# Splitting the router's gate of an attention and expert kernel into three rounds of 4, 2 and 2 batches

## The reference, cut to what matters

```python
x = x + attention(layernorm(x), ctx)          # x: (8 batches, 128 tokens, 256); 32 heads, 8 groups of keys
flat = layernorm(x).reshape(1024, 256)
xm = layernorm(x).mean(axis=1)                # one row for each batch
h1 = gelu(xm @ te_W1.T + te_b1)
task_dist = softmax(h1 @ te_W2.T + te_b2)     # 4 domains
dom = task_dist @ affinity.T                  # 64 values for each batch
logits = flat @ Wr.T + 0.5 * dom              # 64 experts
_, idx = top_k(logits + router_bias, 4)
w = softmax(logits)[idx]; w = w / (w.sum() + 1e-8)
out = sum of w * (silu(x @ Wg[e]) * (x @ Wu[e])) @ Wd[e] over the 4 experts e of a token
out = out + two shared experts of width 256, for every token
x = x + out
```

## Time and profile before

| | |
|---|---|
| median of three executions | 324.55 us (321.69 to 328.14) |
| the profiled execution | 324.12 us, its span 322.1 us |
| PE busy | 250.3 us, 78% of the span |
| DVE, ACT, POOL busy | 176.0, 137.1, 98.7 us |
| mean granted clock of PE | 0.896 |

### The profile page before, as it was taken

The page is one execution under the profiler, slowest core; times in us unless marked ns, Lnnn a source line. Parts: engine busy times, 40 slices in busy tenths (PEclk is TensorE's granted clock), DMA queues, the critical chain, the costliest instruction groups (busy, mean ns, idle before and its releaser), DMA issues.

```text
span 322.1 us, 6518 instructions
## 1 busy us (share of the span) xinstructions
PE 250.3 (78%) x2298; PEld 180.0 (56%) x2298; DVE 176.0 (55%) x441; ACT 137.1 (43%) x326; POOL 98.7 (31%) x188
## 2 busy tenths in 40 slices
PE   3687999999999879998699602999999949759100
PEld 2555567677676555886478401877777716535000
DVE  4468678788787634842058590134355403523943
ACT  2237779678678562433010500533466503512000
POOL 5316404203202011167701772000000262272472
PEclk9999999999999987999689955899999976996855
DMA  6903347437569053662200225589999974763642
GB/s 172 314 7 98 133 135 260 141 126 255 188 215 381 4 195 128 265 228 114 98 19 17 98 98 173 171 246 266 296 277 312 287 225 125 221 177 118 217 143 81
DMA packets 43871, 56.55 MB, mean 176 GB/s; under 512 B 4348, under 2 KB 39744, under 8 KB 42816
## 3 DMA queue, kind: packets, MB, share of 16 engines
q1 hardware_dynamic: 32064, 39.37, 37.8%
q0 software_dynamic: 3072, 8.39, 8.0%
q10 hardware_dynamic: 8704, 8.39, 7.5%
HBM read 34.12 MB, written 22.02 MB: 174 GB/s over the span
## 4 chain that ended last, share of the span: by engine, by line
PE 58%; issue 25%; DVE 6%; DMA 4%; POOL 2%; ACT 2%; SPq 1%; POOLq 0%; ACTq 0%; DVEq 0%
PE bank L1547 12%; PE bank L1172 10%; PE banks L1563 7%; PE banks L1323 6%; PE banks L1333 5%; PE bank L1313 5%; DMA before_wlo<-in_L_xattn_Wfc 3%; PE bank L1176 2%; PE banks L1172 2%; DVE xb_all L1145 2%; PE bank L1466 2%; PE bank L1484 2%; POOL after_whi L596 1%; DVE mx L808 1%; PE bank L1468 1%
## 5 line engine op out<-in xcount | busy, mean ns | idle before, releaser
L808 DVE TENSOR_REDUCE mx<-bank 128x4 f32<-128x512 f32 x64 | 41.8, 684 | 13.8 <-PE bank L1313 12.9
L596 POOL DMA_INDIRECT after_whi<-y_slots,idx x24 | 23.0, 960 | 82.2 <-DMA y_slots<-after_x 66.3
L1121 DVE TENSOR_TENSOR after_x<-bank,after_x 128x128 f32<-128x128 f32 x32 | 9.3, 292 | 69.0 <-ACT after_x L745 60.8
L641 ACT ACTIVATE before_w<-banks 128x512 f32<-128x512 f32 x64 | 38.3, 617 | 19.8 <-PE banks L1323 19.8
L740 ACT ACTIVATE after_wlo<-bank 128x512 f32<-128x512 f32 x32 | 19.1, 598 | 43.3 <-PE bank L1172 38.2
L587 POOL DMA_INDIRECT x_slots<-x_all,idx x28 | 27.2, 972 | 22.7 <-DVE idx L933 14.4
L1313 PE MATMUL bank<-before_w,before_w 128*128 128x512 f32 x64 | 27.7, 458 | 2.7 <-ACT before_w L635 1.4
L1323 PE MATMUL banks<-before_w,before_w 128*128 128x512 f32 x64 | 28.1, 448 | 0.7 <-ACT before_w L641 0.5
L1172 PE MATMUL bank<-ident,xt_all 128*128 128x128 f32 x64 | 13.3, 330 | 18.3 <-DMA xt_all<-x_slots 17.2
L1547 PE MATMUL bank<-after_wlo,after_wlo 128*64 128x64 f32 x512 | 22.6, 241 | 5.1 <-issue 5.1
L1547 PEld LDWEIGHTS bank<-after_wlo,after_wlo 128*64 128x64 f32 x512 | 19.4, 152 | 9.4 <-issue 7.8
(11 more groups left out here) (217 smaller groups left out, 525.8 us busy)
## 6 DMA issues: line engine op xcount, KB each, us to landing
x_slots<-before_sil SPq DMA_DIRECT2D x8, 1024.0 KB, 4.5
w_all<-gate_up SPq DMA_DIRECT2D x8, 1024.0 KB, 4.8
y_slots<-after_x ACTq DMA_DIRECT2D x32, 256.0 KB
w_all<-down SPq DMA_DIRECT2D x8, 512.0 KB, 5.9
xt_all<-x_slots SPq DMA_DIRECT2D x16, 256.0 KB, 4.1
after_so_far<-x_slots SPq DMA_DIRECT2D x8, 256.0 KB
after_sel<-x_slots SPq DMA_DIRECT2D x8, 256.0 KB
after_sil<-in_L_ffn_Wd SPq DMA_DIRECT2D x32, 64.0 KB
```

The lines of the kernel that those rows point to most:

```text
L596: nc.gpsimd.indirect_dma_start(out=got[b % 4][:, k * D:(k + 1) * D], out_offset=None, in_=y_slots[0:last * QROWS], in_offset=bass.Indirect ...
L641: nc.scalar.activation(Pr[g], ST_ps[g % 2][:], exp, scale=SCALE).then_inc(a_exp, 1)
L808: nc.vector.tensor_reduce(mx[par][:, J * g:J * g + J], S_ps[g % 2][:].rearrange("p (j t) -> p j t", j=J), AX_X, ALU.max).then_inc(v_max, 1)
```

## The change

- The gate works in rounds of 4, 2 and 2 batches. The first round is now settled inside attention: its domain steps in step 6, its choice, ranks and all placing in step 7. The domain steps of the second round run in steps 7 and 8, its choice in step 9. The third round follows with the rest of the second after the loop.
- Router logits are computed and summed for one batch in each of the steps 2 to 9 instead of for four batches together.
- For batches 6 and 7 DVE computes mean and variance of the rows itself and POOL only takes the power; PE turns their rows at the head of steps 8 and 9.
- POOL issues the four indirect DMAs of batch 0 in step 8, and the other 28 after the loop, round by round.
- PE starts the shared experts later: gate product 0 in two parts in step 8, units 1 and 2 in step 9 between the gate's products.
- ACT no longer copies the first round's counts and ranks out of PSUM (`counted`), and three rounds need three gelu and three exp steps of the domains instead of two. The PSUM regions of the gate's products move accordingly.

The core of the diff (every hunk on shapes and PSUM regions alone is cut):

```diff
+ROUNDS = ((0, 4), (4, 6), (6, 8))
+LAST_ROUND = len(ROUNDS) - 1
...
+GATE = tuple((LOGITS, b) for b in range(4)) + named(0, DOMAINS) + ((LOGITS, 4),) + named(0, ("logits",) + CHOICE) + (
+        placing(0, 0) + placing(0, 1) + placing(0, 2) + ((LOGITS, 5),) + placing(0, 3)) + (
+        named(1, DOMAINS) + ((LOGITS, 6),) + named(1, ("logits",) + CHOICE) + placing(1, 0) + named(2, DOMAINS[:3])) + (
+        placing(1, 1) + named(2, DOMAINS[3:5]) + placing(1, 2) + placing(1, 3) + named(2, DOMAINS[5:]) + ((LOGITS, 7),)) + (
+        named(2, ("logits",) + CHOICE) + placing(2, 0) + placing(2, 1) + placing(2, 2) + placing(2, 3)) + (
...
-                if has(n - 2):
+                if has(n - 2) and n < B:
                     k = n - 2
                     pool.wait_ge(v_stats, k + 3)
                     wait(pool, v_x2n, k)
                     deviations(LN2, LN2 + 1, LN_STEPS * (k + 2))
+                if has(n - 2) and n >= B:
+                    pool.wait_ge(v_ln, 2 * (n - B + 1))
+                    nc.gpsimd.tensor_tensor(mean_var[:, 2:3], mean_var[:, 1:2], minus_half[:, 0:1], ALU.pow).then_inc(g_rstd, 1)
...
+                if n_is(n, B):
+                    pool.wait_ge(zero_in, 128)
+                    pool.wait_ge(g_x2, 4)
+                    pool.wait_ge(v_gate, gate_step(("rows of the slots", 0)))
+                    scatter(0)
...
-            pool.wait_ge(zero_in, 128)
-            pool.wait_ge(g_x2, B - 1)
-            for b in range(B):
-                if b % HB == 0:
-                    pool.wait_ge(v_gate, gate_step(("rows of the slots", b // HB)))
+            def scatter(b):
+
                 for k in range(TOPK):
...
+
+            pool.wait_ge(g_x2, B - 1)
+            for h in range(len(ROUNDS)):
+                pool.wait_ge(v_gate, gate_step(("rows of the slots", h)))
+                for b in range(max(1, ROUNDS[h][0]), ROUNDS[h][1]):
+                    scatter(b)
...
-                    if g == 7 and n_is(n, B - 2):
+                    if g == 7 and n_is(n, B - 3):
                         hidden_of_domains(0)
-                    if g == 1 and n_is(n, B - 1):
+                    if g == 4 and n_is(n, B - 2):
                         exp_of_domains(0)
-                    if g == 0 and n_is(n, B):
-                        act.wait_ge(pe_rank, 1)
-                        nc.scalar.activation(counted, bank[1][:], copy).then_inc(a_rank, 1)
-                    if g == 3 and (n_is(n, B) or n_is(n, B + 1)):
-
-                        silu(n - B, (n - B) % 2)
+                    if g == 7 and n_is(n, B - 1):
+                        hidden_of_domains(1)
+                    if g == 3 and n_is(n, B):
+                        exp_of_domains(1)
+                    if g == 5 and n_is(n, B):
+                        silu(0, 0)
+                    if g == 3 and n_is(n, B + 1):
+                        rows_out(B - 1)
...
-            silu(2, 0)
-
-            hidden_of_domains(1)
-
-            exp_of_domains(1)
+            hidden_of_domains(LAST_ROUND)
+            exp_of_domains(LAST_ROUND)
+            for v in range(1, EARLY):
+                silu(v, v % 2)
...
+
+                dve.wait_ge(v_stats, k + 3)
+                nc.vector.bn_aggr(mean_var[:, 0:2], stats[:, LN2].rearrange("p a s -> p (a s)")).then_inc(v_ln, 1)
+                dve.wait_ge(v_ln, 2 * (k - B + 2) + 1)
+                nc.vector.tensor_scalar(mean_var[:, 1:2], mean_var[:, 1:2], EPS, None, ALU.add).then_inc(v_ln, 1)
+                dve.wait_ge(g_rstd, k - B + 3)
+                dve.wait_ge(pe_XT, k)
+                dve.wait_ge(g_x2, k)
+                nc.vector.tensor_scalar(x2n[:], xb_all[:, k * D:(k + 1) * D], mean_var[:, 0:1], mean_var[:, 2:3],
+                                        ALU.subtract, ALU.mult).then_inc(v_x2n, 1)
...
-            def logits_sum(h):
-                dve.wait_ge(pe_lg, h + 1)
-                step((LOGITS, h), nc.vector.tensor_reduce(
-                    lg[:, batches(h), :], LG_ps[h][:].rearrange("p (b m e) -> p b e m", b=HB, m=2), AX_X, ALU.add))
+            def logits_sum(b):
+                dve.wait_ge(pe_lg, b + 1)
+                step((LOGITS, b), nc.vector.tensor_reduce(lg[:, b, :], LG_ps.rearrange("p (m e) -> p e m", m=2), AX_X, ALU.add))
...
                     k = n - 2
                     dve.wait_ge(x_rest, 16)
-                    wait(dve, g_ln, LN_STEPS * (k + 2))
+                    wait(dve, g_ln, LN_STEPS * (min(k, B - 3) + 2))
                     dve.wait_ge(v_x2, k + 1)
                     statistics(LN2, xb_all[:, bass.ds(k * D, D)]).then_inc(v_stats, 1)
+                    if n >= B:
+                        own_rows(k)
...
                 if n_is(n, B - 1):
-                    domains_in(0)
+                    logits_whole(0)
+                    choose(0)
                 if n_is(n, B):
-                    place(0, 0)
+                    domains_in(1)
+                if n_is(n, B + 1):
+                    hidden(0, 0)
+                    logits_whole(1)
+                    choose(1)
...
                     if g == 2 and has(n - 1):
                         normalise(n - 1)
-                    if g == 2 and n_is(n, B - 1):
+                    if g == 3 and n_is(n, B - 2):
+                        domains_in(0)
+                    if g == 5 and n_is(n, B - 2):
                         domains_out(0)
+                    if g == 6 and n_is(n, B - 2):
+                        domains_turned(0)
                     if g == 3 and n_is(n, B - 1):
-                        domains_turned(0)
+                        place(0, 0)
                     if g == 5 and n_is(n, B - 1):
-                        logits_whole(0)
-                        choose(0)
-                    if g == 6 and n_is(n, B - 2):
-                        logits_sum(0)
+                        place(0, 1)
+                    if g == 6 and n_is(n, B - 1):
+                        place(0, 2)
+                    if g == 2 and n_is(n, B):
+                        domains_out(1)
                     if g == 5 and n_is(n, B):
-                        place(0, 1)
-                        place(0, 2)
-                    if g == 0 and n_is(n, B + 1):
+                        domains_turned(1)
+                    if g == 7 and has(n - 2) and not n_is(n, B + 1):
+                        logits_sum(n - 2)
+                    if g == 7 and n_is(n, B - 1):
                         place(0, 3)
...
-            hidden(2, 0)
-            domains_in(1)
-            logits_sum(1)
-            hidden(3, 1)
-            domains_out(1)
-            domains_turned(1)
-            logits_whole(1)
-            choose(1)
-            hidden(4, 0)
             place(1, 0)
-            hidden(5, 1)
+            domains_in(2)
             place(1, 1)
+            domains_out(2)
             place(1, 2)
             place(1, 3)
-            hidden(6, 0)
+            domains_turned(2)
+            hidden(1, 1)
+            logits_sum(B - 1)
+            logits_whole(2)
+            choose(2)
+            hidden(2, 0)
+            for part in range(4):
+                place(2, part)
+            hidden(3, 1)
             largest_logit()
-            hidden(7, 1)
+            for v in range(EARLY + 1, SHARED_STEPS):
+                hidden(v, v % 2)
             rows_left(0)
             groups_to_experts()
...
-            def logits(h):
-                pe.wait_ge(v_x2lo, (h + 1) * HB)
-                for i in range(HB):
-                    t = slice((h * HB + i) * T, (h * HB + i + 1) * T)
-                    parts = [(c, xs) for c in range(NC) for xs in (x2hi, x2lo)]
-                    for k, (c, xs) in enumerate(parts):
-                        last = mm(LG_ps[h][:, i * 2 * E:(i + 1) * 2 * E], xs[:, c, t], wrT_hl[:, c].rearrange("p m e -> p (m e)"),
-                                  start=(k == 0), stop=(k == len(parts) - 1))
+            def logits(b):
+                pe.wait_ge(v_x2lo, b + 1)
+                t = slice(b * T, (b + 1) * T)
+                parts = [(c, xs) for c in range(NC) for xs in (x2hi, x2lo)]
+                for k, (c, xs) in enumerate(parts):
+                    last = mm(LG_ps, xs[:, c, t], wrT_hl[:, c].rearrange("p m e -> p (m e)"),
+                              start=(k == 0), stop=(k == len(parts) - 1))
                 last.then_inc(pe_lg, 1)
...
-            def ranks_of_earlier(h):
...
+            def ranks_of_earlier(h, out_):
+                for b in range(ROUNDS[h][0]):
+                    mm(out_.rearrange("p (r e) -> p r e", e=E), ones[:],
+                       sel[:, b * E:(b + 1) * E].rearrange("p (a e) -> p a e", a=1).broadcast_to([P, size(h), E]),
+                       start=(b == 0), stop=False)
...
                 if v == SHARED_UNITS:
-                    pe.wait_ge(v_gate, gate_step((LOGITS, 1)))
+                    pe.wait_ge(v_gate, gate_step(("slots", 1)))
+                    pe.wait_ge(v_gate, gate_step((LOGITS, B - 1)))
```

(92 more changed lines are left out.)

265 lines of the change are left out of this document (133 added, 132 removed).

## The result

The changed kernel took 336.03 us (median of four, 334.43 to 338.16), the kernel before 326.33 (321.69 to 328.14) beside it. The ratio is 1.040, 95% interval 1.027 to 1.054. The forecast was 321 (313 to 330).

A forecast was written before the change was run, and what follows sets the result against it. PE was taken to bound attention and routed experts, with a hole before the first routed multiply in reach. Terms +2.2 + 2.0 - 1.5 - 4.1 + 7.4 - 7.7 - 1.8 = -3.5 gave 320.6, as median 321, range 313 to 330.

The forecast's parts named there:

- The loss under the scatter: PE's shared experts while POOL scatters: time lost between 0 and 5.9 us, taken as 2.
- rival C: Slower, chance 0.14: at least four small hand-overs among DVE, PE and ACT each stall 4.63 us under the scatter; +12.7, or 333.
- The sign I had set for it: PE's last shared product ending later than 195, with DVE or ACT idle on finished PE work.
- The rest of that term: PE behind batch 7's turned rows: work 41.2, waits 3.0, clock 1.2, besides the scatter loss; 47.4 against 40.0, +7.4 us.
- +2.2 for the logits: Steps 2 to 5, bound by PE: each grows 0.45 us for batchwise logits, about 0.1 where DVE's extra sum precedes the maxima.
- +2.0 for step 6: Router products leave (-1.35), domain products come (+2.3), and gelu and exp table loads fall here (+1).
- -1.5 for step 7: Domain waits leave, choice and placing of round 0 come on DVE: 14 us against 15.5.
- Steps 8 and 9: Batch 6's residual sum to batch 7's turned rows: 11.1 us against 15.2, -4.1, with placing gone and shorter moments.
- The hole: PE's last shared product to first routed multiply: 14.3 us instead of 22.0, -7.7, with DVE's weights and 32 register loads left.
- -1.8 for work done ahead: In the hole PE turns three steps and multiplies two ahead, saving 1.8 us.
- Rival B: Hardly any price on PE, chance 0.29: no scatter loss, waits filled, clock up, tables hidden; 313.5 us, range 310 to 317.
- Rival D: Scatter still ends last, chance 0.07: round 2's table later than about 187, time about 325 us.

The follow-up runs named there:

- pool_moments: Changed kernel with POOL's seven steps for the row moments of batches 6 and 7 put back: 339.77 us, ratio 1.042 to the kernel before.
- hold_all: Changed kernel with the 28 transfers after the loop held until the last round's rows of the slots: 345.8 us, ratio 1.066 to the kernel before.
- twice_logits: Changed kernel with every batch's router products issued twice: 336.96 us, one execution.
- half_tokens: Changed kernel with each scatter transfer cut to the first 64 of its 128 tokens, for timing only: 337.70 us, one execution.
- hold_after8: Changed kernel with 8 transfers after the loop sent at once, the other 20 held until the last round's choice: 338.47 us, ratio 1.047 to the kernel before.
- markers: Changed kernel with three small instructions that only mark time, two on DVE and one on ACT: 335.86 us, one execution.
- hold_after12: Changed kernel with 12 transfers after the loop sent at once, the other 16 held until the last round's choice: 337.67 us, ratio 1.044 to the kernel before.
- narrow: Changed kernel with each scattered row cut to half its bytes, written to a tensor of its own, for timing only: 334.29 us, one execution.
- spaced: Changed kernel with two small unread POOL additions ahead of each of the 20 transfers behind batch 0: 330.85 us, one execution.

## Why the prediction was wrong

**The step that failed** is "The loss under the scatter lies between 0 ... and 5.9 ... so I take 2, nearer the first". It measured 13.2 us on PE (the gap before 167.64), and the clock, at 0.61 from 164 to 182, cost more: 61.2 us behind the turned rows against 47.4. The lower end was a misreading. I took the stretch 164 to 182 for work "under the second scatter", but the earlier trace rows put that scatter's start at 175.26, and PE was done 6.6 us later. The shared products never met that burst at a greater age. The next result after them, 7.1 us into it, was even 1.5 us late, done at 182.34 and taken here (the same step takes 0.11 us in the changed kernel, with no burst):

```profile
183.88 0.21 DVE L947 TENSOR_SCALAR erow<-bank 1x64 int32<-1x64 f32 x1 [1.86 <-PE bank L1502]
```

The upper end came from a burst of 16 and was carried to one of 20. The observation that settles it stood in rival C as evidence against C: that the stalls began only 11 us after the scatter did. The new order put its hand-overs just there, 8 to 13 us into the burst.

**Rival C** had the mechanism and nearly the price (333). Its count was wrong: not four hand-overs of 4.6 us, but one of 1.8 and one of 13.2 that ended with the burst. I gave it 0.14; the 4.63 and 11.44 us in the earlier trace rows deserved more than that. The sign I had set for it came: a PE end later than 195 (204.19), with DVE idle on finished work.

**The rest of that term held.** With the scatter paced, the last shared product ends 48.4 us behind the turned rows; I had summed 47.4.

**Steps 2 to 7.** +2.2 for the logits measured +2.7: 0.54 to 0.66 in three steps and 0.99 in the fourth. +2.0 for step 6 measured +2.5, -1.5 for step 7 measured -2.3. The first residual sum, which I had left where it was, comes at 50.37 instead of 49.04; in the eleven other runs with this start it came at 48.88 to 50.67, so part of these 1.3 us is the spread of the runs.

**Steps 8 and 9.** -4.1 measured -3.1 (batch 6's sum to batch 7's 9.0 instead of 8.1, moments and layernorm 2.1 instead of 2.0). The split was wrong: I gave 2.8 us to the placing that left and 1.3 to the moments. pool_moments shows the moments alone carry 3.6: 2.4 in step 8, 1.2 in step 9.

**The hole.** 14.3 forecast, 13.1 measured. The DVE loads of 32 registers (the gap before the multiply) took 2.44 us against 2.2. By the Trainium skill, Runtime: NRT & Kernel Launch, section "Instruction fetch mechanics", with its some 200 ns each, they would by estimate have taken 6.4; no trace here bears that out for registers loaded from the core's own memory. What was late next was DVE's weights, as said. The -1.8 for work done ahead did not show, +0.4 was measured behind the first multiply: from 217 to 223 the granted clock was 0.53, where the kernel before had 1.00 from 203.8 on. No run separates the two.

**Rival B** leaned on the rule in the same section of the Trainium skill that fetching instructions is mostly hidden. DVE's marks ran on time under the burst, up to 154.48, so the trace does not contradict the rule there, but nothing here measures fetches. The stall was real, and it sat in PE's signal.

**Rival D** came up in part: round 2's table was ready at 181.92, yet SP loaded slots at 193.49, before PE was through.

## What to carry to other kernels

Before you move work under a long row of indirect transfers, look in the trace at how old each burst is when engines hand results to one another, and not only at busy shares; a clean stretch counts only if it lay as deep in a burst. Holding the burst back moved the loss; cutting it into pieces of eight with pauses all but removed it, and in the kernel before one pause in the first burst did. And when a bound is taken away, sum what its neighbours did under its cover, for they go where it went.

## What the runs showed of the hardware

- PE's signals to DVE and ACT come late once POOL has issued indirect transfers without a pause, at one in 1.2 to 1.27 us. A result 7.4 us into a burst was on time (hold_all). The domain logits of the last round, done 8.3 to 8.4 us into theirs, were 0.2 to 2.4 us late in eight kernels (twice_logits and half_tokens at the ends, 1.8 in the changed kernel). Later in a long burst it was 9.8 us at 10.1 (hold_after8), 8.0 at 11.9 (hold_all), 13.0 at 12.8 (the changed kernel), 15.9 at 11.8 (markers).
- The burst's age alone does not fix the size: 7.1 us into its second burst the kernel before had a result 1.5 us late, 11.6 us into its first one that was 4.4 late, and a result 9.9 us into a burst of eight, just as it ended, was on time (hold_after8). After a pause of 5.8 us behind twelve transfers a result was 2.2 us late at 7.8 us into the next burst (hold_after12).
- The last late result was taken between 1.1 us before the burst's end (narrow) and 4.6 us after it (hold_all).
- Signals of ACT and DVE to PE were on time under it, within 0.06 us at 20 us and more into a burst (hold_all), and DVE took ACT's within 1.4 us (markers).
- Half the bytes or half the rows did not help; at one transfer in 2.60 us nothing was late, in one execution (spaced).
- What in a transfer delays the signal (its descriptors' writing, its completions) stays open; no run separates these.
- POOL's time for an indirect transfer hardly depends on its rows: 0.96 us for 128 rows, 0.89 for 64, 0.30 between two.
